# A fused attention and mixture kernel: value products of two key tiles issued back to back, and the split maxima transposed as a 128-column tile

## The reference, cut to what matters

```python
# A: 16 heads of 8
att = softmax(where(causal, q @ k.T * 8**-0.5, -inf))        # q, k rotated
x = x + (att @ v) @ wp.T + bp
# F: 8 heads of 64, no mask
v = einsum('bthe,btek->bhtk', topk_mask(gl_v, 2) * sigmoid(gl_v), xv)
attn = softmax(q * scale @ k.T) @ v
out = einsum('bthe,bthk,ekd->btd', topk_mask(gl_o, 2), attn, Wo)
x = x + out
```

## Time and profile before

| | |
|---|---|
| median of 3 runs | 2078.11 us (2077.97 to 2079.36) |
| profiled execution | 2074.39 us |
| its span, first to last instruction | 2072.6 us (1.8 us lie around it) |
| PE busy | 1816.3 us, 88% |
| DVE busy | 1580.1 us, 76% |
| ACT busy | 1273.3 us, 61% |
| POOL busy | 1047.0 us, 51% |
| granted PE clock, mean | 0.967 |

### The profile page before, as it was taken

The page is one execution under the profiler, slowest core; times in us unless marked ns, Lnnn a source line. Parts: engine busy times, 40 slices in busy tenths (PEclk is TensorE's granted clock), DMA queues, the critical chain, the costliest instruction groups (busy, mean ns, idle before and its releaser), DMA issues.

```text
span 2072.6 us, 32651 instructions
## 1 busy us (share of the span) xinstructions
PE 1816.3 (88%) x11328; PEld 881.0 (43%) x11328; DVE 1580.1 (76%) x2934; ACT 1273.3 (61%) x2803; POOL 1047.0 (51%) x1124
## 2 busy tenths in 40 slices
PE   1658999989999898989999998999999899998775
PEld 0223443535444353535444453544435354443332
DVE  4538787888878788788888888887878888787461
ACT  0335757576675757566675756667575766758461
POOL 1223556363645646374655636465563636455433
PEclk8879999999999999999999999999999999999986
DMA  3231203112121302113120211213021121200000
GB/s 97 48 36 32 37 29 43 35 26 30 37 37 42 36 30 33 23 37 36 42 37 30 40 33 27 33 39 37 29 44 35 26 29 37 36 17 14 11 1 6
DMA packets 87617, 68.71 MB, mean 33 GB/s; under 512 B 10720, under 2 KB 83104, under 8 KB 87328
## 3 DMA queue, kind: packets, MB, share of 16 engines
q1 hardware_dynamic: 87456, 66.62, 17.5%
HBM read 32.51 MB, written 10.49 MB: 21 GB/s over the span
## 4 chain that ended last, share of the span: by engine, by line
PE 64%; DVE 13%; ACT 10%; POOL 6%; DMA 3%; issue 3%; SPq 0%; POOLq 0%; DVEq 0%; ACTq 0%; PEldq 0%
PE Y L463 11%; PE M L556 5%; POOL Z L1069 5%; PE S2a L428 5%; ACT Pq L683 5%; PE S1c L404 5%; PE S2b L428 4%; DVE nmaxF L848 4%; PE M L593 3%; PE S1b L404 3%; PE M L514 3%; PE M L489 3%; DMA Ks<-parts 3%; DVE ztmp L930 3%; PE Y L454 2%
## 5 line engine op out<-in xcount | busy, mean ns | idle before, releaser
L1069 POOL TENSOR_TENSOR Z<-Z,ztmp 128x1280 f32<-128x1280 f32 x112 | 324.5, 2897 | 327.9 <-DVE ztmp L958 326.8
L1036 POOL TENSOR_SCALAR_AFFINE_SELECT PT<-PT 128x256 f32<-128x256 f32 (+1 forms) x640 | 254.5, 409 | 386.6 <-ACT PT L668 383.5
L1060 POOL TENSOR_TENSOR Vf<-Vf,ztmp 128x512 f32<-128x512 f32 x256 | 349.0, 1363 | 102.2 <-DVE ztmp L930 93.6
L668 ACT ACTIVATE PT<-S2a 128x512 f32<-128x512 f32 x320 | 191.6, 599 | 170.6 <-PE S2a L422 166.2
L463 PE MATMUL Y<-PT,Vf 128*64 128x512 f32 x1024 | 274.8, 617 | 0.0
L672 ACT ACTIVATE PT<-S2a 128x512 f32<-128x512 f32 x256 | 153.6, 600 | 158.5 <-PE S2a L428 155.7
L930 DVE TENSOR_TENSOR ztmp<-xv,wv_s 128x512 f32<-128x512 f32 x256 | 238.0, 930 | 2.8 <-POOL Z L1069 2.8
L404 PE MATMUL S1c<-Kf,Qf 64*128 64x512 f32 x352 | 203.6, 659 | 36.2 <-ACT Pq L683 32.2
L404 PE MATMUL S1a<-Kf,Qf 64*128 64x512 f32 x352 | 204.5, 662 | 20.6 <-ACT Pq L683 20.6
L668 ACT ACTIVATE PT<-S2b 128x512 f32<-128x512 f32 x320 | 191.5, 598 | 26.3 <-PE S2b L422 26.0
L404 PE MATMUL S1b<-Kf,Qf 64*128 64x512 f32 x320 | 182.8, 652 | 9.5 <-ACT Pq L683 9.5
(11 more groups left out here) (108 smaller groups left out, 3760.7 us busy)
## 6 DMA issues: line engine op xcount, KB each, us to landing
Qs<-parts SPq DMA_DIRECT2D x96, 128.0 KB
Ks<-parts SPq DMA_DIRECT2D x96, 128.0 KB
tab_s<-in_tab SPq DMA_DIRECT2D x16, 512.0 KB, 4.5
xr<-out_x SPq DMA_DIRECT2D x32, 256.0 KB, 2.9
out_x<-res SPq DMA_DIRECT2D x32, 256.0 KB, 2.2
wa_s<-in_wa SPq DMA_DIRECT2D x16, 320.0 KB, 3.1
xl<-out_x SPq DMA_DIRECT2D x16, 256.0 KB, 3.0
out_x<-in_x SPq DMA_DIRECT2D x8, 256.0 KB, 4.4
```

The costliest lines, as they stand in the source:

```text
L668: nc.scalar.activation(PT[:, slot % 2, b, :], t[:, :], ACT.Exp, scale=SCALE_A).then_inc(exps_done.sem, 1)
L1036: last = nc.gpsimd.affine_select(out=v, in_=v, compare_op=ALU.is_ge, fill=0.0, base=0, pattern=pattern, channel_multiplier=-1)
L1060: nc.gpsimd.tensor_tensor(Vf[:, i, :, :], Vf[:, i, :, :], vtmp[:, n % VBUF, :, :], ALU.add).then_inc(v_acc.sem, 1)
L1069: nc.gpsimd.tensor_tensor(Z[:, :, :, :], Z[:, :, :, :], ztmp[:, hh % 2, :, :, :], ALU.add).then_inc(z_acc.sem, 1)
```

## The change

The products of key tiles 0 and 1 are both issued in step 3, and those of tiles 2 and 3 both in step 7, in place of one product in each of the steps 1, 3, 5 and 7. And `nmb` becomes the first 32 columns of a tile of 128 columns, zeroed once at the start; the transpose in `rows` takes the whole tile, and ACT copies the same 32 rows as before.

```diff
-        nmb = sb("nmb", [P, 2, GA, NT], BF)
+        nmb_wide = sb("nmb", [P, P], BF)
+        nmb = nmb_wide[:, 0:2 * GA * NT].rearrange("p (j h t) -> p j h t", j=2, h=GA)
...
-        dve_init = Signal("dve_init", 6)
+        dve_init = Signal("dve_init", 7)
...
-                    nc.tensor.transpose(t[:, :].bitcast(BF)[0:2 * GA * NT, 0:P],
-                                        nmb[:, :, :, :].rearrange("p j h t -> p (j h t)"),
+                    nc.tensor.transpose(t[:, :].bitcast(BF)[:, 0:P], nmb_wide[:, :],
                                         identb[:, :]).then_inc(is_full(use), 1)
...
-                        if b % 2 == 1 and b < 2 * NT:
+                        if b in (3, 7):
+                            values(slot, b // 2 - 1)
                             values(slot, b // 2)
...
-            dve.wait_ge(dve_init.sem, 5)
+            nc.vector.memset(nmb_wide[:, :], 0.0).then_inc(dve_init.sem, 1)
+            dve.wait_ge(dve_init.sem, 6)
```

## The result

| | before | after |
|---|---|---|
| median | 2078.74 us (4 runs, 2077.97 to 2080.10) | 2094.47 us (4 runs, 2093.79 to 2096.72) |
| profiled execution | 2074.39 us | 2096.72 us |

The ratio is 1.0077, with a 95% interval from 1.0061 to 1.0093. The change costs 15.7 us at the median. The forecast was 2085.6 with a range from 2060 to 2100, and "slower" as the likeliest sign.

A forecast was written before the change was run, and what follows sets the result against it. PE is busiest (88%), but runs in step with DVE in places and waits for POOL or ACT in others. Slot terms summed to +0.5 us an iteration, times 15 is +7.5 us: median 2078.1 to 2085.6, range 2060 to 2100.

The forecast's parts named there:

- What a second product costs: A value product directly behind another costs 0.86 us instead of 1.01; each pair saves 0.30 us of array switching.
- the 3.7 us that PE was to lose: PE work saved per iteration: 2.4 in slots 6, 7, 0, 1, 1.2 in slots 2 to 5, 0.15 from the wide transpose.
- Slots 6, 7 and 0: PE still waits for DVE's f_mix or maxima, then pays 0.86 behind: about +0.3, +0.55 and +0.8 us.
- Slot 1: POOL's chain for Z starts sooner, behind DVE's product instead of a mask: about -0.5 us.
- Slots 2 and 3: PE's waits for ACT cover part of the doubled product: -0.15 and -0.55 us.
- Slot 4: ACT and PE take turns; 0.86 comes ahead of step 4, only 0.16 to 0.2 covered: about +0.65 us.
- Slot 5: Step 6 scores move up until `Pq` stops them, about 0.4 net; step 7's doubled product hardly shows: -0.6 us.
- The whole gain: Faster rival: saved switches arrive in slots 6, 7 and 0, -3.25 us an iteration, 2029 us; chance 0.08.
- a slot 0 that doesn't wait: Faster rival: step 4 maxima done by 882.4, slot 0 gains 0.6 instead of losing 0.8, 2064.5 us; chance 0.15.
- nothing moves: Same-time rival: errors of some 0.2 us per term can bring +7.5 us to zero, 2074 to 2082; chance 0.20.
- Less is given back: Slower rival: slot 1's -0.5 missing, slots 2, 3, 5 give half: +1.65 an iteration, 2103 us; chance 0.15.
- the likeliest case: The forecast itself, slower by the summed slot terms, spanning 2082 to 2094 us; chance 0.42.

The follow-up runs named there:

- the light kernels: Kernel before, f_mix cut to one token tile of four, POOL's value additions to one head of eight: single products 2034.15 us; pairs in slots 0, 4 (first), 6, 7 2022.64 us.
- the kernel with four slots: Against the kernel before, pairs in steps 3 and 7 of slots 1, 2, 3 and 5 only, narrow transpose kept: 2040.16 us, ratio 0.9820.

## Why the prediction was right, and where its sizes were off

**What a second product costs.** 0.86 was taken, 0.86 was measured (1.87 less 1.01). The 0.30 of switching saved per pair was too high. Where nothing waits, in the light kernels, two pairs give 0.43, 0.51 and 0.39 us in slots 6, 7 and 0, so 0.20 to 0.26 a pair. One place where the 0.30 is missing is step 1 of slot 6. The product has gone from between two groups of transposes, and the first group takes 0.59 us to the next start, which is no less than the 0.53 or 0.54 that it took ahead of a product:

```profile
947.34 0.60 PE L431 MATMUL S2b<-ident,Pq 128*128 128x128 f32 x4
947.93 0.66 PE L505 MATMUL M<-ident,xn 128*128 128x128 f32 x4
```

Of the 3.7 us that PE was to lose, 2.33 went. Why no more is saved wasn't tried. The error cost the forecast little, because the waits take what is saved. That the array "drains" on a change of tiling mode, as the Trainium skill says in "TensorEngine Tiling (Array Packing)", section Key Properties, agrees with a saving of 0.20 to 0.26; the light kernels turn it into time in slots 6, 7 and 0 and the full ones don't.

**Slots 6, 7 and 0.** Predicted +0.3, +0.55 and +0.8 by waits for DVE; measured +0.31, +0.64 and +0.83. Two experiments show the cause and don't only agree with it: without DVE's load the same pairs give -0.43, -0.51 and -0.39, and in slot 0 the pair moved ahead of the wait gives -0.39 at full load. The waits were forecast at 0.8 ahead of the gate, 0.6 ahead of the projection and 1.3 in slot 0, and read 0.49, 0.50 and 1.15.

**Slot 1.** Predicted -0.5, measured -0.48. POOL's first addition starts 3.27 us into the slot (904.58 less 901.31), where it was 3.76 (890.99 less 887.23), and what it waits for is DVE's product:

```profile
904.58 2.90 POOL L1072 TENSOR_TENSOR Z<-Z,ztmp 128x1280 f32<-128x1280 f32 x1 [0.57 <-DVE ztmp L961]
```

**Slots 2 and 3.** -0.15 and -0.55 predicted, -0.16 and -0.62 measured. In slot 2 the wide transpose takes back 0.12 of the 0.28 that the pairs alone give.

**Slot 4, mis-sized.** The term was +0.65 and the slot cost +1.67. The mechanism held as far as it went: the scores of step 4 come 0.62 later (951.97 less 946.12, against 938.52 less 933.29), their wait for `Pq` is gone, and with light load the pair costs 0.63.

```profile
951.97 0.69 PE L406 MATMUL S1b<-Kf,Qf 64*128 64x512 f32 x1
```

What the term left out is a second effect: a start 0.62 later changed how DVE's multiplications and POOL's additions overlap, and DVE's three grew by 1.02. I had priced DVE's work in this slot as fixed.

**Slot 5, mis-sized the other way.** The term was -0.6, measured -0.93 (-0.86 where slot 4 is left alone). The scores of step 6 start 9.70 us into the slot, where it was 10.64:

```profile
970.75 0.69 PE L406 MATMUL S1c<-Kf,Qf 64*128 64x512 f32 x1
```

They came forward by 0.94, close to the bound that the prediction named, the end of `Pq` (0.98 ahead of the old start, 957.20 less 956.22), and the slot's end came with them. The net of 0.4 for this step was too low; why the doubled product of step 3 costs nothing beside it was not tried alone.

**The sum.** +0.5 an iteration was predicted, +1.27 measured; slots 4 and 5 make up +0.69 of the difference of 0.77. The count of 15 iterations was no good stand-in for the rest. In the two profiled executions 13 iterations are alike, and 13 x 1.27 is 16.5 us. The first iteration, in which the slots fill up, is 6.2 us longer after (157.98 against 151.74), and the last seven slots are 4.4 longer (129.38 against 124.95). Against this, single slots of the kernel before last longer than their median, 4.9 us in all, and 0.2 us in the kernel after. That gives 22.4 us between the spans. Between the medians it is 15.7, since the profiled execution was a short one of the kernel before (2074.39 against a median of 2078.74) and a long one of the kernel after (2096.72 against 2094.47).

**The clock, put at nothing.** The prediction left the clock alone because no wait would be longer than those of before. The iteration that was read bears this out, but two other parts of the time don't. The first slot 6, and the long stretch near the end (slot 1 of the last iteration), have the same number of instructions on PE before and after (62 and 188), at a lower granted clock after. Columns as in the earlier trace rows, before and after in turn:

```profile
97.10:106.91 9.81, 8.70 (x62) 3.16 (x61) 3.27 (x10) 6.44 (x13) 3.27 (x9) 1.00 0.01 3
97.02:109.20 12.18, 10.22 (x62) 3.58 (x61) 3.27 (x10) 6.45 (x13) 3.27 (x9) 0.86 0.01 2
...
1944.44:2014.66 70.22, 44.74 (x188) 20.46 (x189) 41.49 (x57) 33.89 (x84) 29.37 (x20) 0.78 0.03 8
1962.62:2036.17 73.55, 48.43 (x188) 22.60 (x189) 40.85 (x57) 33.65 (x84) 29.38 (x20) 0.72 0.03 8
```

Not all of this is the edit's: the kernel with the first pair in slot 4 alone has the order of before in this slot 6, and took 11.35 us there at a clock of 0.85. The other part of the time goes the other way. In the steady iterations of the kernel before the clock falls to 0.5, the 1.2 GHz level, three times for 3.4 us: twice at the end of slot 1, behind PE's waits for Z (1.33) and for ACT (0.31), and once around the start of slot 4. This is the first, a slot 1 of 14.89 us in place of 13.54, in which matmuls of line 404 take 1.22 in place of 0.69 (its window, then two lines of PE's timeline):

```profile
1243.60:1258.49 14.89, 13.03 (x99) 6.22 (x100) 14.57 (x35) 8.49 (x16) 11.64 (x18) 0.90 0.06 21
...
1255.30 0.85 PE L581 MATMUL M<-ident,Z 128*64 128x128 f32 x4 [0.31 <-ACT parts L659]
1256.08 1.22 PE L404 MATMUL S1c<-Kf,Qf 64*128 64x512 f32 x1
```

The kernel after has none of these falls, and neither has any of the other four kernels with pairs in slots 1, 2 and 3; the nine without them have one to five each. So part of the gain of the kernel with four slots (29 us by its slots, 36 at the median) can be the clock's. What decides between fall and no fall is open: PE idles more in the kernel after than before (11.0 against 7.4 us an iteration), and the kernel with pairs in steps 3 and 6 of slot 0 has one fall although its slot 1 is that of before. No run changes the clock by itself.

**The rivals.** The whole gain and a slot 0 that doesn't wait are refuted by the 1.15 us wait in it, and "nothing moves" by the interval, whose lower end is 1.0061. "Less is given back" lies nearest to the time, but not by its mechanism: slots 1, 2, 3 and 5 gave back 2.19, more than the 1.8 predicted. The direction and the waits of slots 6, 7 and 0 were right by their mechanism. That 2094.47 lies within 2060 to 2100 owes something to luck: it is at the upper edge (2094) of the likeliest case, the sum for an iteration was too small by 0.77, and two things that the prediction did not weigh partly cancel, the longer ends of the program (+10.6) and the long single slots that are gone (-4.7).

## What to carry to other kernels

Putting like array shapes together saves the switch (0.20 to 0.26 us a pair here), but it also moves work from ahead of a wait to behind it, and what it moves is paid in full there: 0.86 against the 0.20 to 0.26 that a pair saves. So ask of each place which side of the next wait the block lands on, and choose by slot: the whole change costs 15.7 us, its pairs alone 9.3 us, and the pairs in the four slots where a wait covers them gain 36 us (2040.16 against 2076.62 on the same chip). A place that gains alone can lose its gain next door, when the two are bound by the same engine, as slots 6 and 7 seem to be. And read the ends of the program too, not only one steady iteration: here they cost 10.6 us beside the 16.5 of the 13 iterations between them.

## What the runs showed of the hardware that was not expected

- Short waits of PE can be followed by a stretch at the lower clock. The kernel before has three of 3.4 us at 0.5 in its steady iterations, each with 1.4 to 1.6 us more in the slots around it; the five kernels with pairs in slots 1, 2 and 3 have none. The 17 executions of the kernel before on one chip run from 2074.11 us at a mean clock of 0.967 to 2082.14 at 0.960.
- DVE and POOL stretch each other, and which of them pays depends on which starts when. A 128x512 f32 multiplication on DVE takes 0.68 us alone. Against POOL's addition of the same size it took 1.15 with the addition at 1.69, or 1.37 to 1.56 with the addition at 1.27. A shift of 0.62 us turned one into the other, in the whole change and in the kernel with slot 4's first pair alone.
- A transpose of 128 columns of bfloat16 in place of 32 loads its weights in the same time, 95 and 96 ns on average, as the groups of PE's weight loads in the kernels before and after show:

```profile
L476 PEld LDWEIGHTS M<-identb,nmb 128*32 128x32 bf16 x64 | 6.1, 95 | 30.3 <-issue 30.1
```

```profile
L478 PEld LDWEIGHTS M<-identb,nmb 128*128 128x128 bf16 x64 | 6.1, 96 | 44.6 <-issue 44.4
```
